# Mask added to the attention scores by two matmuls on TensorE instead of an addition on DVE

## What is computed

```python
q = q * cos + _rotate_half(q) * sin
k = k * cos + _rotate_half(k) * sin
scores = jnp.einsum('bhqd,bhkd->bhqk', q, k) * inv_sqrt_d
scores = scores + attention_mask                  # [batch, 1, 128, 128], 0 or -1e9
w = jax.nn.softmax(scores.astype(jnp.float32), axis=-1)
attn_output = jnp.einsum('bhqk,bhkd->bhqd', w, v)
a_scores = jnp.einsum('bhqd,bhkd->bhqk', q, a_k) * inv_sqrt_d
a_scores = jnp.tanh(gate) * jax.nn.softmax(a_scores, axis=-1)
```

## Time and profile before

| | |
|---|---|
| median of 3 runs | 2524.99 us (2516.36 to 2528.28) |
| the profiled execution | 2524.06 us, its span 2522.1 us |
| attention phase, first to last `mT` copy | 73.50 to 1945.48 us |
| expert phase | from about 2040 us on |
| TensorE matmuls busy | 2069.4 us (82%) |
| DVE busy | 1444.9 us (57%) |
| ACT busy | 1258.6 us (50%) |
| POOL busy | 821.0 us (33%) |
| mean granted TensorE clock | 0.914 |

### The profile page before, as it was taken

The page is one execution under the profiler, slowest core; times in us unless marked ns, Lnnn a source line. Parts: engine busy times, 40 slices in busy tenths (PEclk is TensorE's granted clock), DMA queues, the critical chain, the costliest instruction groups (busy, mean ns, idle before and its releaser), DMA issues. The chain is left out here.

```text
span 2522.1 us, 55300 instructions
## 1 busy us (share of the span) xinstructions
PE 2069.4 (82%) x18953; PEld 1234.9 (49%) x18954; DVE 1444.9 (57%) x3715; ACT 1258.6 (50%) x2260; POOL 821.0 (33%) x851
## 2 busy tenths in 40 slices
PE   4888888888788877878788888888888449999997
PEld 2455555544444444544444444544445226666664
DVE  4567666666666666666666666666666433333332
ACT  4565555555555555555455555555555234444443
POOL 2123323233233222232223232222222334444443
PEclk7899989899889888998898989899999769999999
DMA  2001111000000000010000000000001234444444
GB/s 101 21 29 32 30 35 47 29 29 29 29 29 29 29 29 29 29 29 29 29 29 29 29 29 29 29 29 29 29 25 20 52 85 83 84 83 84 83 84 66
DMA packets 69810, 105.95 MB, mean 42 GB/s; under 512 B 25024, under 2 KB 29120, under 8 KB 69120
## 3 DMA queue, kind: packets, MB, share of 16 engines
q0 software_dynamic: 24096, 37.51, 8.6%
q1 hardware_dynamic: 45536, 65.69, 8.4%
HBM read 67.51 MB, written 35.65 MB: 41 GB/s over the span
## 5 line engine op out<-in xcount | busy, mean ns | idle before, releaser
L515 ACT ACTIVATE pr<-st 128x512 f32<-128x512 f32 x512 | 305.0, 596 | 451.0 <-PE st L1083 335.1
L1051 PE MATMUL md<-kk,qz 128*128 128x128 f16 x2048 | 221.1, 248 | 203.1 <-DVE mx L714 79.9
L379 POOL TENSOR_TENSOR t<-t 128x512 f32<-128x512 f32 x64 | 81.4, 1271 | 872.1 <-DVE t L692 872.1
L710 DVE TENSOR_REDUCE mx<-md 128x4 f32<-128x512 f32 x256 | 176.5, 689 | 299.0 <-remote 218.9
L1097 PE MATMUL av<-pr,vv 128*17 128x128 f32 x4096 | 253.6, 293 | 66.4 <-issue 56.1
L1051 PEld LDWEIGHTS md<-kk,qz 128*128 128x128 f16 x2048 | 136.1, 108 | 314.3 <-issue 169.4
L1431 PE MATMUL y<-w1s,hgT 128*128 x1704 | 280.3, 315 | 4.6 <-ACT hgT L1345 4.6
L414 POOL DMA_INDIRECT lists<-row,posi x256 | 248.8, 972 | 86.4 <-issue 86.4
L1074 PE MATMUL st<-qz,kk 128*128 128x256 f16 x1024 | 204.9, 283 | 41.8 <-DVE mT L735 37.1
L507 ACT ACTIVATE qz<-ma 64x256 f16<-64x256 f16 x512 | 191.8, 375 | 79.8 <-remote 65.8
L1431 PEld LDWEIGHTS y<-w1s,hgT 128*128 128x128 f16 x1704 | 164.5, 98 | 96.6 <-issue 5.1
(11 more groups left out here) (200 smaller groups left out, 3875.0 us busy)
## 6 DMA issues: line engine op xcount, KB each, us to landing
wst<-in_w SPq DMA_DIRECT2D x32, 352.0 KB, 3.1
cin<-in_ctx SPq DMA_DIRECT2D x32, 256.0 KB, 4.1
xin<-in_x SPq DMA_DIRECT2D x32, 256.0 KB, 3.8
xres<-in_x SPq DMA_DIRECT2D x32, 256.0 KB, 3.8
out<-x SPq DMA_DIRECT2D x32, 256.0 KB, 2.1
h_pairs<-ohs SPq DMA_DIRECT2D x32, 256.0 KB
lists<-row,posi POOLq DMA_INDIRECT x256
msk<-in_mask SPq DMA_DIRECT2D x32, 64.0 KB, 3.6
```

The costliest lines, as they stand in the source:

```text
L515: act.activation(pr[:, path, :, :], st[path][:, :, :], ACT.Exp).then_inc(p_ex.sem, 1)
L710: dve.tensor_reduce(mx[:, 1, 4 * g:4 * g + 4], sm[1][:, :, :], AX.X, ALU.max).then_inc(s_ad.sem, 1)
L1051: i = pe.matmul(sm[path][:, j, :], qz[:, h // 2, h % 2, :], keys[:, h // 2, :], start=True, stop=True)
```

## The change

The two matmuls of `mskp` and the identity are put in front of the direct scores of the own path, as the first of one accumulation over the whole bank: here the identity is stationary and the mask's part moving, repeated four times, since queries are on the partitions. The addition on DVE and its semaphore go. TensorE waits for both parts of the mask at group 0. The load of the mask no longer waits for DVE's maxima, as DVE reads `msk` for them no more.

```diff
-    s_mask = ev("s_mask", GROUPS)
...
             source = dram["mask"](n)
             sp.wait_ge(m_lo.sem, m_lo.at(n.shift(-2)))
-            sp.wait_ge(s_own.sem, s_own.at(n.shift(-2)))
             sp.dma_start(msk[:, n.par, :], source).then_inc(m_in.sem(n), 16)
...
             dve.tensor_reduce(mx[:, 1, 4 * g:4 * g + 4], sm[1][:, :, :], AX.X, ALU.max).then_inc(s_ad.sem, 1)
-            dve.tensor_tensor(sm[0][:, :, :], sm[0][:, :, :], msk[:, n.par, :].unsqueeze(1).to_broadcast([P, 4, P]),
-                              ALU.add).then_inc(s_mask.sem, 1)
-            dve.wait_ge(s_mask.sem, s_mask.at(n, g + 1))
             dve.tensor_reduce(mx[:, 0, 4 * g:4 * g + 4], sm[0][:, :, :], AX.X, ALU.max).then_inc(s_own.sem, 1)
...
             if g == 0:
                 pe.wait_ge(r_lg.sem, r_lg.at(n.shift(-2)))
+                pe.wait_ge(m_lo.sem, m_lo.at(n))
+                pe.wait_ge(m_hi.sem, m_hi.at(n))
             for path, keys, used in ((1, akst, s_ad), (0, kst, s_own)):
                 pe.wait_ge(used.sem, used.at(n, g))
+                if path == 0:
+                    for part in range(2):
+                        pe.matmul(sm[0][:, :, :], identr[:, :],
+                                  mskp[:, n.par, part, :].unsqueeze(1).to_broadcast([P, 4, P]),
+                                  start=(part == 0), stop=False, skip_group_check=True)
                 for j in range(4):
                     h = 4 * g + j
                     i = pe.matmul(sm[path][:, j, :], qz[:, h // 2, h % 2, :], keys[:, h // 2, :],
-                                  start=True, stop=True)
+                                  start=(path == 1), stop=(path == 1 or j == 3), skip_group_check=True)
```

## The result

The changed kernel takes 2554.56 us (median of 4 runs, 2552.57 to 2556.08), the kernel before on the same chip 2526.64 us (median of 4, 2516.36 to 2531.44). The ratio is 1.0116 with a 95% interval of 1.0083 to 1.0148: slower by about 1.2%. The forecast was 2540 us, within 2496 to 2574. The profiled execution took 2556.08 us, its span 2554.1 us against 2522.1; the mean granted clock is 0.932 against 0.914.

What follows compares the result with a forecast made beforehand. In attention a TensorE-DVE ring bounds each batch's second part, with a stall tied to POOL's scatters in 29 batches. Stalled batches +46, clock -29, prologue -1 give +16 us: 2524 + 16 = 2540 us, range 2496 to 2574.

Steps and rivals of the forecast that it cites:

- The forecast as summed: Whole kernel: slower, 2540 us as summed, taken as 2528 to 2560 us, chance 0.31.
- The ring at full clock: Attention, u = 9 to 15, TensorE and DVE alternating by group: a turn takes 2.34 us (2.44 with open load) against 2.52.
- The 0.54 us from `L1078`: Cost of the added matmul pair per group, read from the same tiles with operands exchanged; the Trainium skill gives 0.43 us.
- The scatters and the stall's end: In 29 stalled batches, POOL's list scatters and the end of DVE's wait at group 4 move 0.98 us later.
- Groups 5 to 7 at 1.2 GHz: Turns behind the stall at half clock: group 5 unchanged, group 6 +0.7 us, group 7 gets 0.1 back; +0.6 a batch.
- The clock's return: Value projection after the groups: the pairs fill TensorE's gaps, full clock returns in 18 slow batches, 18 x 1.6 = -29 us.
- The fixed place of the stall: DVE's group 4 goes on about 2.7 us after POOL's last scatter starts, hanging on TensorE's progress at u = 11.
- A: Rival: group 4's signal gets through before the last scatter, the stall ends earlier; faster, 2498 us, chance 0.25.
- B: Rival: no gain of clock, slow value projections stay; +46 to +55 us, 2573 us, chance 0.22.
- C: Rival: earlier signals or part of the clock's gain pay for the rest; within 12 us of 2524 us, chance 0.22.

Runs made afterwards that it cites:

- the three pairs without the stall in the ring: Kernels before and after, in order: list scatters moved early (ratios 1.0199, 1.0038), scatters spread in four pairs (1.015, 0.9989), both unchanged on the third chip (1.0003, 0.9933).
- both: Changed kernel with DVE's addition and its wait put back, mask counting as zero, first chip: 2649.07 us, ratio 1.0363 to the kernel before.
- neither: Changed kernel without the two mask matmuls and without DVE's addition, mask counting as zero, first chip: 2420.99 us, ratio 0.9485 to the kernel before.
- early_after: Changed kernel with POOL's eight list scatters put ahead of its norm work for the batch after next, first chip: 2563.52 us, 1.0038 to the kernel before.
- after_again: The changed kernel, unaltered, run again on the third chip: 2346.94 us, ratio 0.9933 to the kernel before.
- before_again: The kernel before, unaltered, run again on the third chip: 2366.08 us, ratio 1.0003.

## Why the prediction was right, and what it missed

The forecast as summed came in: slower, by about 1.2%, with 2554.56 us inside its own range of 2528 to 2560. The change itself is nearly twice what was summed: +28 us in the medians and +32 in the profiled spans, against +16. By its steps:

**The ring at full clock: right.** Forecast 2.34 us a turn (2.44 with the load open), measured 2.35. The groups of a clean batch were forecast at 26.60, 29.75, 32.66, 35.00, 37.34, 40.48, 42.82 and 45.16 us after `mT`; they came at 26.58, 29.72, 32.59, 34.93, 37.28, 40.42, 42.78 and 45.13. The batch is 0.28 us shorter (forecast 0.25). The 0.54 us from `L1078` was the right choice over 0.43.

**The scatters and the stall's end: right in the middle, too small in the sum.** The first scatter was forecast 0.98 us later, and is 1.0 (31.91 to 32.92); group 4 comes at 44.5 us instead of 43.5. But the sum to the stall's end is +39.9 us instead of +28. The scatters' shift itself gives 29 x 1.04 = 30 us of it. The rest is at the heads of the loop passes, in every second batch, where the loop starts anew. There TensorE waits before `L1076` for 1.7 us or more in each of twelve batches, with either kernel (0.98 us in a batch without a loop head). These twelve waits are 22.3 us in sum before and 25.9 after: +3.6. Behind four of them after (2.0 to 2.8 us long) the clock is granted at 0.50 (in 1433 to 1436, for one), which before does not happen in the first half of any batch, and group 0 comes another 1.3 to 1.6 us later: +6.2. I had not looked at this wait. On the third chip the same twelve waits are longer with either kernel (up to 7.4 and 10.8 us), so it is no property of the changed kernel that I can show, and whether the longer program brings it on is open.

**Groups 5 to 7 at 1.2 GHz: right.** Forecast +0.6 us a batch; measured +19.3 / 29 = +0.67. Group 6 has TensorE as its releaser and comes 3.5 to 4.0 us after group 5 in most batches (forecast 3.4). The sum is partly luck, since it also holds the further stalls before group 6, which the forecast left as they were: steps of over 4.4 us from group 5 to 6 stand in nine batches before and in seven after, and not in the same ones. A batch's median from group 4 to 7 went from 8.54 to 9.41 us, +0.87.

**The clock's return: right in kind, too large.** This is the term of the sum that was mis-sized most on the side of the gain. The forecast let all 18 slow projections that it counted go. There were 19 in the batches with scatters and 20 of 31 in all (over 3.2 us), and 8 are left. So 12 went, each worth 21.7 / 12 = 1.8 us of tail: the price was right and the number too high, and the tail gives back 21.7 us instead of 29. The pair fills the gap in most batches but not where a further stall stands before group 6. That it is the change that brings the clock back, and not chance, is shown by the three pairs without the stall in the ring (22 to 0, 15 to 2, 21 to 5), by the mean granted clock of all their runs (0.899 to 0.906 against 0.922 to 0.929, 0.941 to 0.944 against 0.958 to 0.965, 0.938 to 0.948 against 0.954 to 0.961), and by both, where the pair stands beside DVE's addition (20 to 10); neither, where DVE's addition alone is gone, has 26. What one projection less is worth varies, though: 39.1 / 22 = 1.8 us of tail in the first pair, 10.5 / 16 = 0.7 us in the third.

**The fixed place of the stall: wrong as a rule, right for this change.** I took its end as tied to the end of the scatters. The kernel without the pair goes on 7.1 or 8.6 us after the first, and not 11.6. With the pair (after, both) it is 11.5 to 11.6 in the medians. What I had right is that TensorE's signals are late while the scatters run, and not stopped: the rows at 1531.49 and 1538.27, and the router's in early_after, show it. The engine's own halts on "issue" come on top (53.1 us before the values in the kernel after, none in after_again). What makes the signals late, and whether the engine halts for the same cause, is open. The waits at the heads of the loop may be another thing. In the wait of 2.52 us that ends at 1556.34 the only DMA traffic is a packet of a queue of kind "instruction" (DMA view, 1553.9 to 1556.4: packets, MB, share of 16 engines):

```profile
q14 instruction: 1, 0.01, 1.3%
```

That is a hint of a program that comes late, and no proof. During the scatters such a packet decides nothing, since it stands there with the stall (from 1531.94 in the kernel after, 2.90 us) and without it (from 1396.12 in before_again, 3.30 us). Why some chips have the stall at group 4 and others have not stays open too.

**The rivals.** A did not happen: group 4 starts 11.5 to 11.7 us after the first scatter in 26 of 29 batches with either kernel, and the early ones are the same two (8.7 and 5.4 us before, 8.8 and 4.4 after; the third exception is the last batch, whose scatters begin at 20.9 us). B did not either: the clock came back. C's even exchange isn't this chip's either. On the third chip, which has no stall at group 4 to lengthen, the change is 0.7% faster, by the clock and the shorter turns.

The errors have one sign: 12 us up to the stall's end, 2 us behind it, 7 us of clock not returned. What lies behind the last `mT` gave 4.4 us back: +16 became +32.

## What to carry to other kernels

Work moved from one engine of a ring to the other is worth the exchange inside the ring (0.72 us for 0.55) only where nothing else sets the end; here the engine that got the work also set the time of eight scatters three turns later, and each microsecond there went one to one into a stall. Look for what hangs on the fuller engine's progress before counting the saving of the emptier one. And work that fills TensorE's gaps has a value that no busy time shows: the tail behind them ran at full clock more often, worth 10 to 39 us in the three pairs of kernels without the stall in the ring.

## What the hardware showed unexpectedly

The same two kernels differ by chip in level and in sign: before takes 2526.64 us beside the result and 2556.0 us on the first chip of the experiments, but 2361.14 and 2365.15 us on the second and third, and the change's ratio is 1.0116 beside the result and 0.9933 on the third. Most of the difference lies in one place, signals of TensorE that come late while eight indirect DMAs of 128 entries run at a pitch of 1.26 us: 2.9 us in the median on the chip of the result, 0.01 us on the third, with the same scatters (group 3 to 4 in the kernel before: 8.1 us against 2.5).

The lateness follows the scatters: with the first scatter at 31.9 or 32.9 us after `mT` on such a chip, the wait for the late signal ended 2.7 us behind the start of the last one in 26 of 29 batches; with the first at 20.9 to 26 us it ended 1.2 to 2.8 us behind it in most.

At the head of each of twelve loop passes TensorE waits 1.7 to 10.8 us before its first matmul, against 0.98 us in a batch without a loop head, on every chip seen.
